# A fifth of the calls moved in the hand-written lists of five engines, in a gated linear attention layer with a ternary feed-forward network

## What is computed

```python
q, k, v = x @ Wq, x @ Wk, x @ Wv              # 16 heads of 8
g = sigmoid(x @ Wf + bf)
def step(state, (qt, kt, vt, gt)):            # over the 1024 tokens of a sequence
    state = state * gt[..., None] + vt[..., None] * kt[..., None, :]   # 8x8 for each head
    return state, einsum('bhij,bhj->bhi', state, qt)
out = norm(out) * gamma + beta
x = layernorm(x + (out * silu(x @ Wg)) @ Wout)
h = silu(tlin(x, w1)) * tlin(x, w2)           # 128 -> 512, weights ternary times a scale
h = gelu(tlin(h, h1)); h = gelu(tlin(h, h2))  # 512 -> 512
x = layernorm(x + tlin(h, w3))                # 512 -> 128
```

## Time and profile before

| | |
|---|---|
| median of 3 runs | 509.78 us (507.11, 509.78, 509.82) |
| span of the profiled execution | 505.3 us |
| PE busy | 495.5 us, 98% |
| PE weight loads, beside it | 383.7 us, 76% |
| DVE busy | 447.2 us, 89% |
| ACT busy | 405.6 us, 80% |
| POOL busy | 310.0 us, 61% |
| DMA | 79.47 MB, queue of SP 63.7% of 16 engines |

### The profile page before, as it was taken

How to read it: one execution, slowest core, us unless ns; L and a number is a source line. 1 busy time by engine, 2 the same in 40 slices (tenths; PEclk the granted TensorE clock), 3 DMA queues, 4 the chain that set the end, 5 groups by cost and what they waited for, 6 DMA issues and landing times.

```text
span 505.3 us, 8095 instructions
## 1 busy us (share of the span) xinstructions
PE 495.5 (98%) x2528; PEld 383.7 (76%) x2528; DVE 447.2 (89%) x708; ACT 405.6 (80%) x839; POOL 310.0 (61%) x362
## 2 busy tenths in 40 slices
PE   8999999999999999999999999999999999999997
PEld 6667787877878787777877777787777778687896
DVE  4999899999999999999999999899999999994171
ACT  5677788887897877879798787989878797978955
POOL 0842839577392948748394875748486584928423
PEclk9999999999999999999999999999999999999999
DMA  7999989718079976698897790880797592520001
GB/s 257 226 252 240 208 215 221 194 48 205 0 187 227 244 180 134 155 219 197 190 237 180 178 236 3 189 208 1 169 225 168 138 210 71 121 67 1 22 3 65
DMA packets 43372, 79.47 MB, mean 157 GB/s; under 512 B 4928, under 2 KB 5952, under 8 KB 43072
## 3 DMA queue, kind: packets, MB, share of 16 engines
q1 hardware_dynamic: 43040, 78.61, 63.7%
q10 hardware_dynamic: 288, 0.33, 0.2%
HBM read 11.81 MB, written 4.19 MB: 32 GB/s over the span
## 4 chain that ended last, share of the span: by engine, by line
PE 69%; DVE 9%; issue 8%; POOL 8%; ACT 3%; SPq 2%; DMA 1%; POOLq 0%; ACTq 0%; DVEq 0%
PE F L2301 41%; PE back L2402 8%; PE front L2202 6%; DVE KJ L1557 4%; PE back L2287 2%; POOL h1lo L441 2%; PE back L2186 2%; PE ps_v L2202 2%; POOL h2lo L441 2%; PE back L2269 2%; SPq L283 2%; POOL KJ L502 1%; PE F L2198 1%; DMA QJ<-qk 1%; DVE h L1621 1%
## 5 line engine op out<-in xcount | busy, mean ns | idle before, releaser
L441 POOL TENSOR_TENSOR h1lo<-h,h1hi 128x512 fp32r<-128x512 f32 x60 | 76.4, 1290 | 18.5 <-ACT h1hi L864 18.2
L871 ACT ACTIVATE h<-F,cols 128x512 f32<-128x512 f32 x120 | 80.5, 686 | 8.6 <-PE F L2301 7.6
L441 POOL TENSOR_TENSOR h2lo<-h,h2hi 128x512 fp32r<-128x512 f32 x60 | 76.1, 1290 | 10.6 <-ACT h2hi L864 10.4
L1557 DVE TENSOR_TENSOR_SCAN KJ<-g,carry,KJ 128x512 f32<-128x512 f32 x64 | 78.3, 1264 | 0.3 <-ACT g L803 0.2
L1557 DVE TENSOR_TENSOR_SCAN KJ<-g,KJ 128x512 f32<-128x512 f32 x64 | 74.3, 1203 | 0.4 <-ACT g L803 0.3
L508 POOL TENSOR_TENSOR QJ<-QJ 128x512 f32<-128x512 f32 x14 | 18.0, 1283 | 91.6 <-DVE QJ L1572 91.6
L2301 PE MATMUL F<-h2hi,whi 128*128 128x512 f32 (+1 forms) x256 | 72.1, 417 | 0.7 <-ACT h L871 0.5
L1564 DVE TENSOR_TENSOR QJ<-QJ,KJ 128x1024 f32<-128x1024 f32 x60 | 71.4, 1213 | 1.0 <-DMA QJ<-qk 0.8
L2301 PE MATMUL F<-h1hi,whi 128*128 128x512 f32 (+1 forms) x256 | 70.7, 414 | 1.0 <-DVE h L1621 0.8
L2301 PE MATMUL F<-h1lo,whi 128*128 128x512 f32 (+1 forms) x256 | 67.7, 401 | 0.2 <-POOL h1lo L441 0.2
L2301 PE MATMUL F<-h2lo,whi 128*128 128x512 f32 (+1 forms) x256 | 66.4, 402 | 0.0
(11 more groups left out here) (182 smaller groups left out, 937.9 us busy)
## 6 DMA issues: line engine op xcount, KB each, us to landing
KJ<-qk SPq DMA_DIRECT2D x120, 256.0 KB, 4.8
QJ<-qk SPq DMA_DIRECT2D x120, 256.0 KB, 4.8
x_in<-in_x SPq DMA_DIRECT2D x16, 256.0 KB, 4.7
xT<-in_xT SPq DMA_DIRECT2D x15, 256.0 KB, 5.0
out<-res SPq DMA_DIRECT2D x15, 256.0 KB, 2.0
wraw<-in_wffn SPq DMA_DIRECT2D x2, 1024.0 KB, 8.8
wraw<-in_wffn SPq DMA_DIRECT2D x2, 256.0 KB, 4.7
wproj<-in_wproj SPq DMA_DIRECT2D x2, 192.0 KB, 3.7
```

The costliest lines, as they stand in the source:

```text
L441: e.tensor_tensor(h_lo[layer][:, t, :w], h[:, t, :w], h_hi[layer][:, t, :w].bitcast(f32), ALU.subtract).then_inc(lo_done[layer], 1)
L871: e.activation(dst[:, t, :WIDTH[n]], F[t][:, :WIDTH[n]], ACT.Gelu, scale=scale[t]).then_inc(gelu_done[layer], 1)
L1557: e.tensor_tensor_scan(K, g[:, :WIDTH[n]], K, init, ALU.mult, ALU.add).then_inc(scan_done, 1)
```

## The change

The same calls, with the same operations and buffers, stand in another order in all five lists; about a fifth of them moved, most by one to three places. Two edits are of another kind: in fetch() the waits that only the first half (half 0) made are now made by both halves, and the wait for wproj_landed[0] moved from the list of PE into project() for tile 0. The diff, cut to the calls of which the prediction speaks:

```diff
                 e.dma_start(xT[n % XTB][:, :WIDTH[n]], xT_d[:, tokens(n)]).then_inc(xT_landed[n % XTB], 16)
 
             def fetch(n, which, half):
-                if half == 0:
-                    if which and n == 2:
-                        e.wait_ge(qsj_done, len(QS_VECTOR))
-                        e.wait_ge(qsj_gp_done, len(QS_GP))
-                        e.wait_ge(carry_done, 1)
-                    elif which and n > 2:
-                        e.wait_ge(qs_done, NPAIR * (n - 2))
-                        e.wait_ge(carry_done, n - 1)
-                    elif n > 1 and not which:
-                        e.wait_ge(oT_made, n - 1)
+                if which and n == 2:
+                    e.wait_ge(qsj_done, len(QS_VECTOR))
+                    e.wait_ge(qsj_gp_done, len(QS_GP))
+                    e.wait_ge(carry_done, 1)
+                elif which and n > 2:
+                    e.wait_ge(qs_done, NPAIR * (n - 2))
+                    e.wait_ge(carry_done, n - 1)
+                elif n > 1 and not which:
+                    e.wait_ge(oT_made, n - 1)
...
-            fetch(1, 1, 1)
+            load_weights(3)
             fetch(1, 0, 0)
-            load_x(0)
-            load_weights(3)
             fetch(1, 0, 1)
+            load_x(2)
+            fetch(2, 1, 0)
+            fetch(2, 1, 1)
             load_xT(4)
-            fetch(2, 1, 0)
-            load_x(2)
+            fetch(2, 0, 1)
             load_x(1)
-            fetch(2, 1, 1)
             fetch(2, 0, 0)
+            fetch(3, 1, 1)
             fetch(3, 1, 0)
-            fetch(2, 0, 1)
             load_xT(5)
-            fetch(3, 1, 1)
-            fetch(3, 0, 0)
             fetch(4, 1, 0)
             fetch(3, 0, 1)
+            fetch(3, 0, 0)
             fetch(4, 0, 0)
+            fetch(4, 1, 1)
             load_x(3)
             fetch(4, 0, 1)
+            store(0)
+            load_xT(6)
+            load_xT(7)
...
+            load_x(11)
             store(7)
-            fetch(12, 1, 1)
-            fetch(12, 0, 1)
-            load_x(11)
+            fetch(12, 0, 0)
+            fetch(13, 0, 1)
+            fetch(13, 1, 1)
             fetch(13, 1, 0)
-            fetch(13, 1, 1)
             store(8)
             store(9)
+            load_x(12)
             fetch(13, 0, 0)
+            load_x(13)
             fetch(14, 1, 0)
-            load_x(12)
             fetch(14, 1, 1)
-            fetch(13, 0, 1)
-            fetch(15, 1, 0)
-            load_x(13)
+            fetch(15, 1, 1)
             fetch(14, 0, 0)
             fetch(14, 0, 1)
-            fetch(15, 1, 1)
             load_x(14)
             load_x(15)
+            fetch(15, 1, 0)
             store(10)
+            fetch(15, 0, 1)
             fetch(15, 0, 0)
-            fetch(15, 0, 1)
             store(11)
...
-            scale_w3()
...
+            scale_w3()
...
             rstd_2(1)
+            gated_y(3)
             lo(2, 2, 0)
-            gated_y(3)
             lo(2, 2, 1)
...
-            kv_gp(10, 6)
             lo(1, 8, 0)
             lo(1, 8, 1)
             lo(1, 8, 2)
             rstd_of(9, "o")
             lo(1, 8, 3)
+            kv_gp(10, 6)
...
+            hi(2, 7, 0)
             gelu(1, 7, 1)
-            hi(2, 7, 0)
...
+            silu_gate(13)
+            square(10)
             hi(1, 11, 2)
-            silu_gate(13)
...
@@ -1717,12 +1716,12 @@
             gated_y0()
             scan(1, 4)
             residual_1(0)
-            qs(1, 0)
             stats_1(0)
             scan(1, 5)
+            find_low_parts()
             scan(1, 6)
...
@@ -1731,15 +1730,14 @@
             hmul(0, 0)
             hmul(0, 1)
             qs(1, 3)
-            kv(2, 0)
             hmul(0, 2)
             hmul(0, 3)
             stats_o(1)
+            kv(2, 0)
+            scan(2, 0)
             kv(2, 1)
             kv(2, 2)
-            scan(2, 0)
             scan(2, 1)
-            qs(2, 0)
             scan(2, 2)
             scan(2, 3)
             scan(2, 4)
@@ -1748,10 +1746,11 @@
             scan(2, 5)
             scan(2, 6)
             scan(2, 7)
+            qs(2, 0)
             qs(2, 1)
+            qs(2, 2)
             add(2, 0)
             x1_lo(1)
-            qs(2, 2)
             qs(2, 3)
             add(2, 1)
             add(2, 2)
@@ -1763,38 +1762,38 @@
             hmul(1, 2)
             hmul(1, 3)
             kv(3, 1)
+            kv(3, 2)
...
-            residual_1(6)
-            stats_1(6)
             scan(7, 2)
             scan(7, 3)
+            residual_1(6)
...
+            hmul(7, 1)
             residual_2(6)
-            hmul(7, 1)
...
+            scan(11, 5)
             residual_1(10)
             stats_1(10)
-            scan(11, 5)
...
             qs(13, 1)
             qs(13, 2)
+            x1_lo(12)
             add(13, 0)
-            x1_lo(12)
+            qs(13, 3)
             add(13, 1)
...
+                if n == 0:
+                    e.wait_ge(wproj_landed[0], 16)
                 e.wait_ge(xT_landed[n % XTB], 16 * (n // XTB + 1))
                 return e.matmul(bank[:, :WIDTH[n]], weights, xT[n % XTB][:, :WIDTH[n]], start=True, stop=True)
 
...
 
             def rest(low_parts):
                 up_hi(0, 0, low_parts)
+                up_lo(0, 0, low_parts)
                 up_hi(0, 1, low_parts)
-                up_lo(0, 0, low_parts)
...
-                last_begin(0)
                 up_hi(1, 0, low_parts)
                 up_lo(1, 0, low_parts)
+                last_begin(0)
                 last_rest(0)
                 up_hi(1, 1, low_parts)
                 up_lo(1, 1, low_parts)
...
+                project_f(5)
                 mid_lo(2, 1, 1, low_parts)
                 mid_lo(2, 1, 2, low_parts)
                 mid_lo(2, 1, 3, low_parts)
+                last_begin(1)
                 up_hi(2, 0, low_parts)
-                last_begin(1)
...
-                project_q(9)
                 mid_open(1, 6, 2, low_parts)
                 mid_open(1, 6, 3, low_parts)
                 mid_hi(1, 6, 1, low_parts)
                 mid_hi(1, 6, 2, low_parts)
+                project_q(9)
...
+                project_k(12)
                 up_hi(9, 2, low_parts)
                 up_lo(9, 2, low_parts)
                 up_hi(9, 3, low_parts)
-                project_k(12)
                 up_lo(9, 3, low_parts)
                 project_gate(11)
...
+                mid_lo(1, 13, 3, low_parts)
                 mid_open(2, 13, 0, low_parts)
                 mid_open(2, 13, 1, low_parts)
-                mid_lo(1, 13, 3, low_parts)
                 mid_open(2, 13, 2, low_parts)
                 mid_open(2, 13, 3, low_parts)
...
                 tail_lo_products(2, 1, 1, low_parts)
                 tail_lo_products(2, 1, 2, low_parts)
                 tail_lo_products(2, 1, 3, low_parts)
+                last_block(0)
+                last_block(1)
                 last_block(2)
                 last_block(3)
 
             warm_up()
-            e.wait_ge(wproj_landed[0], 16)
             project_0(0)
+            project_v(0)
             project_0(1)
-            project_v(0)
```

More of the change, by code:

```diff
@@ L344, in _ @@
             load_x(3)
             fetch(4, 0, 1)
-            load_x(4)
-            fetch(4, 1, 1)
-            load_xT(6)
-            fetch(5, 1, 0)
-            store(0)
-            fetch(5, 1, 1)
-            load_xT(7)
+            store(0)
+            load_xT(6)
+            load_xT(7)
+            fetch(5, 1, 0)
+            fetch(5, 0, 1)
+            fetch(5, 1, 1)
+            load_xT(8)
+            fetch(5, 0, 0)
+            load_x(4)
+            load_x(5)
+            fetch(6, 1, 0)
@@ L353, in _ @@
             store(1)
-            fetch(5, 0, 0)
-            fetch(5, 0, 1)
-            fetch(6, 1, 0)
             fetch(6, 1, 1)
             fetch(6, 0, 0)
-            store(2)
-            load_x(5)
-            load_xT(8)
+            fetch(6, 0, 1)
+            fetch(7, 1, 1)
             load_xT(9)
             load_x(6)
+            store(2)
             fetch(7, 1, 0)
-            fetch(6, 0, 1)
-            fetch(7, 1, 1)
+            fetch(7, 0, 0)
+            load_xT(10)
             load_x(7)
-            load_xT(10)
@@ L369, in _ @@
-            fetch(7, 0, 0)
             fetch(8, 1, 0)
+            fetch(8, 1, 1)
             fetch(7, 0, 1)
             store(3)
-            fetch(8, 1, 1)
             fetch(8, 0, 0)
+            fetch(9, 1, 1)
+            load_xT(11)
             fetch(8, 0, 1)
-            load_xT(11)
             fetch(9, 1, 0)
+            load_x(8)
+            store(4)
             fetch(9, 0, 0)
-            store(4)
             fetch(9, 0, 1)
-            fetch(9, 1, 1)
+            load_xT(12)
@@ L382, in _ @@
             fetch(10, 1, 0)
-            load_x(8)
-            load_xT(12)
-            fetch(10, 1, 1)
-            fetch(10, 0, 0)
             fetch(10, 0, 1)
@@ L690, in _ @@
             lo(1, 10, 3)
```

(28 more changed lines are left out.)

711 lines of the change are left out of this document (353 added, 358 removed).

## The result

The changed kernel takes 510.73 us (median of 11 runs, 509.75 to 512.81), the kernel before on the same chip 508.23 (11 runs, 507.04 to 509.82). The ratio is 1.0046, with a 95% interval of 1.0031 to 1.0060: slower by 2.3 us. The interval lies above 1, but the difference is just within the 0.5% (2.55 us) that the prediction counts as no change. The forecast was 507.0 with a range of 502.0 to 513.8. The range holds the time; the direction is wrong. With the larger sample the kernel before is also 1.5 us faster than the 509.78 from which the sum started, and the profiled execution of before (505.3 us) was one of its shorter ones, 507.1, so 1.8 us lie around its span, not 4.5. The profiled execution of after took 511.08, with a span of 509.2.

What follows compares the result with a forecast made beforehand. PE (TensorE), busy 98% of the span, was taken as the bound. Losses of 0.7 and 0.2 us less gains of 3.7 gave -2.8, from 509.78 to 507.0 us, with a range of 502.0 to 513.8.

Steps and rivals of the forecast that it cites:

- What bounds the kernel: Whole kernel: PE, busy 98% of the span, is the bound; the change can win only its idling and lost overlap.
- The waits that go: PE's waits in the middle and late tiles, (a) to (e), would shrink or vanish: 3.6 us, 3.7 with roundings.
- The waits that come: PE at tile 1: a new stall of about 1.1 us for x1_lo(1), +0.7 net of the start.
- +0.2 for x1_lo(2): Tile 2: last_begin(1) ahead of up_hi(2,0) and x1_lo(2) one add later would cost 0.2 us.
- The walk with before's durations: All five engines: new lists walked with old durations, asking at each wait what comes first; summed to -2.8 us.
- Rival A: Middle: DVE is the bound, PE's removed waits return at the next hmul or x1lo; 509.5 us, chance 0.17.
- The start: First 43 us: stats_1(0) ahead of qs(1,0) and up_lo(0,0) right after up_hi(0,0) would gain 0.4 us.
- late landing: Tile 2: fetch(2,1,0) behind load_x(2) lands at about 50 to 50.5 instead of 41.5, hidden by kv(2,0)'s later place.
- The tail: Last 25.3 us: same matmuls, transposes and last_block one step later; 0, to -0.2 us.
- The two other edits at nothing: Fetch waits on both halves, and the wproj wait in project of tile 0: 0 each, the first bounded by 4.2 us.
- Rival D: More than the listed waits goes, 4.4 us of DVE's and tighter matmul spacing; 501.5 us, chance 0.05.
- Rival B: Tile 2's K fetch behind load_x(2) lands late, x1_lo late in several tiles; 513.8 us, chance 0.23.

Runs made afterwards that it cites:

- e9: The changed kernel with one DVE call put back, scan(11,1) behind hmul(9,2); the wait at mid_open(1,9,0) went, keeping 0.63 of its 0.85 us.
- e10: The changed kernel with one POOL call put back, rstd_of(3,"1") ahead of lo(2,2,3); up_hi(0,0) to last matmul 457.79 us, against 459.00.
- e14: The changed kernel with SP's first 30 calls as before; ratio 1.0035 to the kernel before.
- e4: The changed kernel with the old lists from mid_hi(2,13,1) on (old tail); 508.1 to 509.0 us four times, 509.7 to 511.3 eight times.
- e7: The kernel before with the edits of e5 and the new tail from mid_hi(2,13,1) on; ratio 1.0047.
- e5: The kernel before with only the fetch waits on both halves and the wproj wait inside project of tile 0; ratio 1.0012.
- e18: The kernel e17 with the tail as before; up_hi(0,0) to last matmul 458.31 us.
- e17: The changed kernel with four engines' first 43 us and SP's first 30 calls old, and the edit of e10; up_hi(0,0) to last matmul 458.45 us.
- e6: The changed kernel with all five lists up to tile 2's up-projection (about 105 us) as before; up_hi(0,0) to last matmul 459.43 us.
- e8: The kernel before with the two edits of e5 and the changed lists from up_hi(11,0) to the tail; up_hi(0,0) to last matmul 458.67 us.
- e11: The changed kernel with the calls of e9, e10 and x1_lo(1) ahead of qs(2,2), and PE's old order around up_lo(6,3) and project_q(9); lost 1.49 us behind the flag.

## Why the prediction was wrong, point by point

**What bounds the kernel: right.** PE's work is the same, and the change moved only its waits and what lies around them.

**The waits that go: right in kind, two thirds in size.** last_begin(11), project_q(9), project_gate(11) and mid_open(2,7,0) no longer wait; mid_lo(1,8,0) and mid_open(2,13,3) wait 0.3 and 0.2 less. attention_out(3) and project_k(15) wait as before. Of the 3.6 us, 2.5 came. (The sum rounded the 3.6 up to 3.7.)

**The waits that come: the step that failed in the middle.** The sum had one, x1_lo(1) with 1.1; it measured 1.2 of idling, 1.46 with the overlap. Four others of 0.6 to 0.85 were not there: transpose_x1(3) 0.72, mid_open(1,6,2) 0.74, mid_open(1,9,0) 0.85, mid_lo(1,9,0) 0.58, 2.9 together. Two have a moved call of 1.2 us ahead of the one that PE waits for (e9, e10). The third lost the matmuls that filled its wait: project_q(9), whose leaving I counted as a gain, had stood in front of mid_open(1,6,2); it moved behind ten matmuls, not one more group as I wrote. For the fourth, POOL's lo(1,9,t), no edit was tried. I walked the places where before waited, and not each place where a call had moved. The prediction's own mark for this, "more than three new PE waits over 0.3", was met. These losses less the 2.5 make +1.9, where the net is +0.73: the other 1.1 are small gains that I had not listed in their places, the largest 0.46 at up_hi(0,2), just behind the start. The +0.2 for x1_lo(2) did not show.

**"The walk with before's durations": the step beneath.** Rival A, with 0.17, described the middle best: waits come back at the next hmul or x1lo. The net there is +0.73, or +0.3 against the mean of three kernels with the old order, where the sum had -2.8 (with -0.4 of it for the start). The runs add a reason for it: of single edits worth 0.63, 1.21 and 0.74, three together were worth 0.70.

**The start: wrong.** I counted -0.4 for it. Up to the flag it is 0.7 longer by the order, and the flag's register load, to which I gave no price and which the waits list calls "issue", took 1.0 on average in place of 0.49. That goes with SP's order around load_x(2) and fetch(2,1,0), the very move that I named as the main loss, by another way than the late landing. The landing cost at most 0.23 (e14, with all of SP's first 30 calls back).

**The tail: wrong.** I had "0, to -0.2" for PE, which is right for PE (-0.1). The price is behind it: a part of the last store is late by 1.2 to 1.8 in every profile with the new tail and in a quarter of those with the old one, so about 1.0 on average by the profiles. The times of pairs say less surely 0.5 (e4 against after) and 1.8 (e7 against e5), and nothing for e18 against e17.

**The two other edits at nothing: right** (e5).

**Rival D: nothing of it.** The 512-column matmuls of product() that wait for nothing start 0.23 us apart in after as in before; the order made none of them tighter.

**Rival B** had the right sign and place, x1_lo(1), but its time, 513.8, took K's fetch and three more x1_lo for late. None of those three was.

Together: +0.3 to +0.7 in the middle, +0.7 and about 0.5 at the start and about +1.0 at the end make 2.5 to 2.9, and the medians differ by 2.5, the ratio says 2.3. It is an estimate from one profile of each kernel, and the share of the end in it is the least sure.

## What to carry to other kernels

When calls move, price every place where a call now stands ahead of one that the bounding engine waits for, not only the waits that the old trace shows; a call that leaves a place may have been the filler of the next wait. In this pipeline, with two engines over 95% busy, gains of single moves didn't add: try them together before counting them. A kernel put together from parts of two orders can lose at the seam what neither order loses (e6, e8, e14). Look also at the two places outside of the engines' busy rows, a register load that all matmuls queue behind, and the last store.

## What the runs showed of the hardware

- PE's register load of a flag in SBUF took 0.49 us in ten profiles, and 0.49 to 1.65 in ten others that differed in what SP had sent just before.
- A 16 KB packet of code behind the last store held a DMA engine for 0.9 to 1.4 us, and in 14 of 20 profiles one of the 16 parts of a 64 KB store with it, which began within 0.02 us of the packet's end and landed 1.2 to 2.4 us after the others.
- After 1.84 us without a matmul and 1.1 us of matmuls at full clock, PE's clock was granted at 0.5 of full speed, the 1.2 GHz level, for 3.4 us in one execution (e11), and stayed at 1.00 behind the same gap in another (after).
- The first two 512-column projection matmuls, behind the 16 of the warm-up, took 1.06 to 1.99 us. They are the longer the later the trace's first clock record, full speed, begins (4.0 to 7.2 us in twenty profiles); the table by stretches reads 1.00 before it too.
